# Four-stage attention kernel for 32 batches: all TensorE products as two halves of 64 partitions, in two lanes

## What is computed

```python
# stage 1: attention, 16 heads of 16, queries from the side input, keys from x and the own position
q = (side + b_self) @ Wq + bq;  k = ((x + b_prev) | (side + b_self)) @ Wk + bk;  v = (x | side) @ Wv + bv
w = softmax(cat(masked(q @ k_prev.T), sum(q * k_self)) / 4)
x = x + (w[:, :-1] @ v_prev + w[:, -1:] * v_self) @ Wo + bo
# stage 2: adapter chosen by an id, then layer norm
a = x + relu(x @ W1[id] + b1[id]) @ W2[id] + b2[id];  x = x + normed(a) * gamma[id] + beta[id]
# stage 3: a linear layer chosen by an id
x = x + x @ W[id].T + b[id]
# stage 4: pooling by scores, under one of three masks
s = tanh(x @ W1 + b1) @ v
x = x + (softmax(where(mask[id], s, NEG)) @ x) / count
```

## Time and profile before

| | |
|---|---|
| median of 3 runs | 934.45 us (933.97 to 934.48) |
| the profiled execution | 936.64 us, its span 935.0 us |
| a step of the loop | 27.44 us (489.60 to 517.04) |
| TensorE, VectorE, ScalarE, GpSimd busy | 97%, 75%, 68%, 64% of the span |
| TensorE's clock | upper level (2.4 GHz) in all 40 slices |
| DMA | 124.54 MB, mean 133 GB/s |

### The profile page before, as it was taken

One profiled execution on the slowest core, in us unless ns is written; L12 is line 12 of the kernel. 1 busy time (PEld: TensorE's weight loads), 2 busy tenths in 40 slices (PEclk: granted clock), 3 DMA queues, 4 the chain that ended last, 5 costly groups with the idle time before them and its releaser, 6 DMA issues.

```text
span 935.0 us, 27514 instructions
## 1 busy us (share of the span) xinstructions
PE 910.3 (97%) x8611; PEld 762.3 (82%) x8611; DVE 704.2 (75%) x1364; ACT 634.4 (68%) x1125; POOL 600.9 (64%) x767
## 2 busy tenths in 40 slices
PE   8999999999999999999999999999999999999887
PEld 7787788888888888888888888888888888887666
DVE  7666777787777787777788777787877777787555
ACT  3456677777667677767777776777776677776643
POOL 4354667767666676666767666677766667764562
PEclk9999999999999999999999999999999999999999
DMA  7444433445443444444344444334444433433231
GB/s 246 152 141 143 136 116 125 145 138 159 141 129 102 151 133 145 160 132 125 107 159 129 149 159 125 124 115 154 135 149 149 121 125 128 152 116 96 71 95 53
DMA packets 113208, 124.54 MB, mean 133 GB/s; under 512 B 23541, under 2 KB 95110, under 8 KB 113158
## 3 DMA queue, kind: packets, MB, share of 16 engines
q1 hardware_dynamic: 111384, 121.22, 41.3%
q10 hardware_dynamic: 1774, 2.68, 0.9%
HBM read 63.99 MB, written 8.96 MB: 78 GB/s over the span
## 4 chain that ended last, share of the span: by engine, by line
PE 89%; issue 5%; DVE 3%; ACT 2%; POOL 1%; DVEq 0%; POOLq 0%; ACTq 0%
PE M L482 28%; PE ST L585 12%; PE PV L564 11%; PE PV L482 10%; PE M L490 7%; PE SN L589 6%; PE M L804 5%; PE M L616 3%; PE M L674 3%; DVE mx L1343 2%; PE M L763 2%; PE M L753 1%; ACT x1T L1029 1%; PE M L497 1%; PE M L641 0%
## 5 line engine op out<-in xcount | busy, mean ns | idle before, releaser
L1343 DVE TENSOR_REDUCE mx<-SN 128x4 f32<-128x1024 f32 x248 | 303.6, 1224 | 102.0 <-PE SN L589 99.4
L1053 ACT ACTIVATE pt<-ST 128x1024 f32<-128x1024 f32 x256 | 262.5, 1025 | 105.0 <-PE ST L585 95.0
L585 PE MATMUL ST<-qst,kst 64*128 64x256 f32 x1024 | 187.7, 305 | 8.6 <-ACT pt L1053 3.5
L585 PEld LDWEIGHTS ST<-qst,kst 64*128 64x128 f32 x1024 | 136.1, 186 | 64.4 <-issue 26.9
L589 PE MATMUL SN<-kst,qst 63*128 63x256 f32 x1008 | 184.0, 304 | 0.7 <-issue 0.7
L589 PEld LDWEIGHTS SN<-kst,qst 63*128 63x128 f32 x1008 | 132.8, 186 | 1.3 <-issue 0.9
L564 PE MATMUL PV<-pt,vaug 128*32 128x256 f32 x2048 | 124.6, 384 | 0.1
L888 POOL TENSOR_TENSOR ss<-xsin,ss 128x512 fp32r<-128x512 f32 x32 | 41.0, 1283 | 122.2 <-ACT ss L1029 114.3
L564 PEld LDWEIGHTS PV<-pt,vaug 128*32 128x32 f32 x2048 | 60.2, 110 | 43.6 <-issue 6.3
L888 POOL TENSOR_TENSOR x2T<-x2f,x2T 128x512 fp32r<-128x512 f32 x31 | 39.9, 1288 | 47.0 <-ACT x2T L1029 47.0
L482 PE MATMUL M<-lwp,x2T 128*128 128x320 f32 x378 | 68.2, 316 | 1.0 <-issue 1.0
(11 more groups left out here) (190 smaller groups left out, 2101.4 us busy)
## 6 DMA issues: line engine op xcount, KB each, us to landing
qst<-qp SPq DMA_DIRECT2D x186, 128.0 KB
kst<-kp SPq DMA_DIRECT2D x186, 128.0 KB
xsin<-in_xsT SPq DMA_DIRECT2D x31, 512.0 KB, 3.4
adw<-in_wad SPq DMA_DIRECT2D x32, 322.5 KB, 3.8
xr<-in_x SPq DMA_DIRECT2D x32, 256.0 KB, 4.1
lwf<-in_lwT SPq DMA_DIRECT2D x32, 256.0 KB, 3.1
pm<-in_pmask SPq DMA_DIRECT2D x31, 257.0 KB, 2.7
out<-ob SPq DMA_DIRECT2D x31, 256.0 KB, 2.2
```

The costliest lines, as they stand in the source:

```text
L585: keys = nc.tensor.matmul(ST[e][:, half * S:half * S + S], kst[par][lo_:lo_ + MROW + 1, pair, half * P:half * P + P], qst[par][lo_:lo_ + M ...
L1053: nc.scalar.activation(pt[:, g, :, j:j + 2, :].rearrange("p h e q -> p e h q"), ST2[:].rearrange("p e (h q) -> p e h q", h=2), ACT.Exp, sc ...
L1343: nc.vector.tensor_reduce(out=mx[odd][:, :, col:col + PH + 1:PH].rearrange("p h e -> p e h"), in_=SN2[:].rearrange("p e (h k) -> p e h k", ...
```

## The change

From step 3 on (`LANES_FROM`) up to step 31 (`LANES_TO` = 32) all engines run a new function `lane_step` in place of `step`; the tail takes over what is left. Steps -2 to 2 are as before.

On TensorE every product and transpose other than scores and weighted sums is cut into two halves along the contraction, partitions 0 to 63 (LOW) and 64 to 127 (HIGH). Both halves add into the same bank, one first and the other later; the second waits on a semaphore (`half_low`, `half_high`) which the first half's last matmul increments. `LANES` holds for each piece its step offset, its bank and which half goes first. `side_by_side` takes two generators, a low lane and a high one, and issues from the lane that has used fewer columns so far, so that two different pieces run beside each other. A transpose's half turns 64 partitions into 64 output columns. `rest(n)` issues nothing; it only counts columns. `weighted` pv1 of batch t-1 now stands first in the step, pv0 ahead of scores 6 as before. The scores blocks are unchanged.

The other engines' queues have the same operations in a new order, and some a step later: the high part `x1Thi`, `x1Tlo` and `x1bT` of batch t-2, `x3` of t-3, `masked`, pooling and `outs` of t-4 are now done in step t. `pool` is two pieces with a bank each. VectorE now waits for both halves of `lin` before either `x3`. The tail gets `masked`, `x3`, `r3`, `outs` of one more batch on VectorE, `srep`, `lin0`, `lin1`, `pT`, `pool` on TensorE (with 8 fillers in place of 10 at one point), and the exponential and its copy on ScalarE.

```diff
+LANES = [
+    ("pv1", -1, 3, None), ("x1T", -2, 1, LOW), ("srep", -4, 2, HIGH), ("v", 1, 0, HIGH), ("ks", 1, 3, LOW),
+    ("h", -2, 2, HIGH), ("k", 2, 1, HIGH), ("num0", -1, 0, LOW), ("num1", -1, 3, LOW), ("q", 2, 2, HIGH),
+    ("ad", -2, 0, LOW), ("pT", -4, 3, LOW), ("aT", -1, 1, HIGH), ("ss", 1, 3, LOW), ("pool0", -4, 0, HIGH),
+    ("pool1", -4, 2, LOW), ("lin0", -3, 1, LOW), ("lin1", -3, 3, HIGH), ("pv0", 0, 2, None), ("x2T", -2, 3, LOW),
+    ("wo", -1, 0, HIGH), ("vs", 1, 1, LOW),
+]
...
+            def side_by_side(low, high):
+
+                halves_left, spent = [low, high], [0, 0]
+                while halves_left != [None, None]:
+                    k = HIGH if halves_left[LOW] is None else LOW
+                    if None not in halves_left:
+                        k = LOW if spent[LOW] <= spent[HIGH] else HIGH
+                    columns = next(halves_left[k], None)
+                    if columns is None:
+                        halves_left[k] = None
+                    else:
+                        spent[k] += columns
...
+                def other_half(name, b):
+
+                    while name not in issued:
+                        yield 64
+                    pe.wait_ge(sem(HALF[LANES[LANE[name]][3]]), halves(name, b))
...
+                def split_rows(name, dsts, left, right, rows):
+
+                    begins, r, last = first_half(name, rows), rows_of(rows), None
+                    for k, dst in enumerate(dsts):
+                        for c in range(NC2):
+                            for x, y in SPLIT:
+                                last = nc.tensor.matmul(dst, left(x, c, k)[r], right(y, c)[r],
+                                                        start=begins and k == c == x == y == 0,
+                                                        stop=not begins and c == 1 and x == 1, skip_group_check=True)
+                                yield dst.shape[-1]
+                    return last
+
+                def turned_rows(dst, src, cols, rows):
+
+                    r, last = rows_of(rows), None
+                    for to, at in cols:
+                        last = nc.tensor.transpose(dst[:, to + 64 * rows:to + 64 * rows + 64], src(at)[r], ident[r, r])
+                        yield 134
+                    return last
...
+                if by_lanes("pv1", t - 1):
+                    vacate("pv1", t - 1)
+                    weighted(lane_bank["pv1"], 1, t - 1, odd)
+                scores(on, t, par, 0)
+                side_by_side(itertools.chain(residual_turned(t - 2, LOW), rest(256), row_scores(t - 4, LOW),
+                                             own_keys(t + 1, odd, LOW)),
+                             itertools.chain(row_scores(t - 4, HIGH), values(t + 1, odd, HIGH),
+                                             residual_turned(t - 2, HIGH)))
+                scores(on, t, par, 1)
+                side_by_side(itertools.chain(values(t + 1, odd, LOW), rest(2000), hidden(t - 2, LOW),
+                                             queries_back(0, t - 1, LOW), queries_back(1, t - 1, LOW)),
+                             itertools.chain(own_keys(t + 1, odd, HIGH), hidden(t - 2, HIGH), keys_(t + 2, par, HIGH)))
+                scores(on, t, par, 2)
+                side_by_side(itertools.chain(keys_(t + 2, par, LOW), adapted(t - 2, LOW), pooled_turned(t - 4, LOW),
+                                             queries(t + 2, par, LOW)),
+                             itertools.chain(queries_back(0, t - 1, HIGH), queries_back(1, t - 1, HIGH),
+                                             queries(t + 2, par, HIGH), rest(1000), pooled_turned(t - 4, HIGH),
+                                             adapted(t - 2, HIGH), attention_turned(t - 1, HIGH)))
+                scores(on, t, par, 3)
+                side_by_side(itertools.chain(own_scores(t + 1, LOW), attention_turned(t - 1, LOW), pooled(1, t - 4, LOW)),
+                             itertools.chain(pooled(0, t - 4, HIGH), rest(300), own_scores(t + 1, HIGH)))
+                scores(on, t, par, 4)
+                side_by_side(itertools.chain(pooled(0, t - 4, LOW), linear(0, t - 3, LOW)),
+                             itertools.chain(pooled(1, t - 4, HIGH), linear(1, t - 3, HIGH)))
+                scores(on, t, par, 5)
+                side_by_side(linear(1, t - 3, LOW), linear(0, t - 3, HIGH))
+                vacate("pv0", t)
+                weighted(lane_bank["pv0"], 0, t, par)
+                scores(on, t, par, 6)
+                side_by_side(itertools.chain(normed_turned(t - 2, LOW), own_values(t + 1, odd, LOW)),
+                             itertools.chain(attention_out(t - 1, HIGH), normed_turned(t - 2, HIGH)))
+                scores(on, t, par, 7)
+                side_by_side(attention_out(t - 1, LOW), own_values(t + 1, odd, HIGH))
```

More of the change, by code:

```diff
@@ L72 @@
 NAMES = [n for _, n, _, _ in PIECES]
+LOW, HIGH = 0, 1
+HALF = ("half_low", "half_high")
+LANES_FROM, LANES_TO = 3, B
+LANES = [
[5 more added lines that the diff above has]
+]
+LANE = {n: k for k, (n, _, _, _) in enumerate(LANES)}
+STEP_OF = {n: o for _, n, o, _ in PIECES}
+STEP_OF.update(pool0=STEP_OF["pool"], pool1=STEP_OF["pool"])
 def done(b, per=1, nth=None):
@@ L92, in before, with by_lanes, halves @@
     return b * UNITS + unit
+def by_lanes(name, b):
+    return not isinstance(b, int) or max(0, LANES_FROM + STEP_OF[name]) <= b < B
+def halves(name, b):
+    _, off, _, first = LANES[LANE[name]]
+    u = b - off
+    own = [(o + (1 if j <= LANE[name] else 0), max(0, LANES_FROM + STEP_OF[m]))
+           for j, (m, o, _, f) in enumerate(LANES) if f == first]
+    if isinstance(u, int):
+        return sum(max(0, min(u + a, B) - start) for a, start in own)
+    return u * len(own) + sum(a - start for a, start in own)
 def block4(nc: bass.Bass, x, xsT, lens, ids, wq, wk, wv, wo, wad, lw, lwT, lb, fixed_d, early_d, kidx_d,
@@ L459, in _ @@
+            steps(sp, step, lane_step)
             step(B, 0, "lwf")
@@ L461, in _ @@
             step(B, 0, "pm")
+            step(B - 1, 1, "out")
             step(B, 0, "lbr")
@@ L524, in _, with weighted @@
                       "lin0": (("x3", 2, 1),), "lin1": (("x3", 2, 2),), "srep": (("masked", 1, 1),),
[1 row of a table removed]
[2 rows of a table added]
                       "pv1": (("pvt", 2, 2),)}
+            def weighted(dst, k, b, i):
+                pe.wait_ge(sem("exp_done"), before(b, 8 * k + 8))
+                pe.wait_ge(sem("v"), done(b))
+                for g in (2 * k, 2 * k + 1):
+                    for kb in range(2):
+                        for j in range(4):
+                            last = nc.tensor.matmul(dst[32 * j:32 * j + 32, (g % 2) * S:(g % 2) * S + S],
+                                                    vaug[i][:, kb, 4 * g + j, :], pt[:, g, kb, j, :],
+                                                    start=kb == 0, stop=kb == 1)
+                last.then_inc(sem("pv_done"), 1)
@@ L554, in free @@
                             return
-                def weighted(k, b, i):
-                    pe.wait_ge(sem("exp_done"), before(b, 8 * k + 8))
-                    pe.wait_ge(sem("v"), done(b))
-                    free(f"pv{k}")
-                    for g in (2 * k, 2 * k + 1):
-                        for kb in range(2):
-                            for j in range(4):
-                                last = nc.tensor.matmul(PV[32 * j:32 * j + 32, (g % 2) * S:(g % 2) * S + S],
-                                                        vaug[i][:, kb, 4 * g + j, :], pt[:, g, kb, j, :],
-                                                        start=kb == 0, stop=kb == 1)
-                    last.then_inc(sem("pv_done"), 1)
@@ L718, in step @@
                     pe.wait_ge(sem("ones1"), 32)
-                scores(0)
+                scores(on, t, par, 0)
                 if go("E", "pv1"):
-                    weighted(1, t - 1, odd)
+                    free("pv1")
+                    weighted(place("pv1", t), 1, t - 1, odd)
                 first = isinstance(t, int) and t == 0
@@ L769, in step @@
                     keys_()
-                scores(4)
+                scores(on, t, par, 4)
                 if on["B"]:
@@ L786, in step @@
                 if on["C"]:
-                    weighted(0, t, par)
-                scores(6)
+                    free("pv0")
+                    weighted(bank["pv0"], 0, t, par)
+                scores(on, t, par, 6)
                 if go("F", "x2T"):
@@ L831, in keep_busy @@
+            steps(pe, step, lane_step)
             def keep_busy(n):
@@ L1009, in _ @@
+            steps(pool, step, lane_step)
             step(B, 0, "eyed")
@@ L1563, in _ @@
+            steps(dve, step, lane_step)
+            step(B - 1, 1, "masked")
+            step(B - 1, 1, "x3a")
             step(B, 0, "x3b")
@@ L1571, in _ @@
             step(B - 1, 1, "x1Tlo")
+            step(B - 1, 1, "r3")
             step(B, 0, "sc")
```

(1 more changed line is left out.)

848 lines of the change are left out of this document (774 added, 74 removed), and 3 rows, old and new, of the table READER.

## The result

The changed kernel takes **955.61 us** (median; 952.26 to 958.21) against 934.47 (933.97 to 936.46) of the kernel before on the same chip: ratio **1.022**, 95% interval 1.0178 to 1.0263. I had forecast 890 with a range up to 926. It is slower where I said faster, and the profiled execution (953.38, span 951.6) shows why in four lines of its page.

A forecast was written before the change was run, and what follows sets the result against it. TensorE was taken as the bound, busy 27.42 of a 27.44 us step. Its 24.6 us plus 1.2 of stalls make 25.8; 936.64 - 47.6 + 3.0 = 892.0, less 2.2 for the median, about 890 us, range 862 to 926.

The forecast's parts named there:

- 29 x 1.64: Steps 3 to 31 each get 1.64 us shorter, 47.6 us in all.
- Halves' own cost: Second halves' semaphore waits and the extra increment for each group of transposes, costed at nothing.
- Borders: Around scores blocks, switching between full and half rows costs 0.37 us a block; eight blocks save 3.0 us a step.
- Products and transposes: In TensorE's lanes, half products cost 0.119 us, pairs' sum unchanged; half transposes cost 0.056, saving 1.4 us a step.
- D: Rival: mixed lanes wait for each other in TensorE's queue; at 30 ns a pair, step 29.2, time 990 us; chance 0.07.
- C: Rival: half transposes cost 0.109 us, so lanes gain nothing there; step 26.8 us, near 919; chance 0.19 together with B.
- E: Rival: halves' weight loads are not hidden, so the 15.6 us of products and transposes nearly double; chance 0.02.
- B: Rival: VectorE's queue order binds, four fullest periods lose 0.25 us more each; step 26.8, 919 us; chance 0.19 with C.
- F: Rival: a bank's reader is late in every section, TensorE waits instead of switching, time stays near 934; chance 0.05.
- A: Rival: nearly no stalls, step 24.6 to 25.1 us, time 862 us; chance 0.14.
- The step of 25.8: Main-loop step: TensorE alone 24.6 us plus 1.2 of stalls, the largest 0.74 ahead of scores 3; 1.64 less than before.
- Ends: First steps stay; the tail takes on a pooling and a linear layer, costing 3 us, bounds 0 and 4.

The follow-up runs named there:

- written out: The changed kernel with TensorE's program alone written out for all steps instead of looping, other engines keeping their loops; 899.95 us, ratio to before 0.9612.
- written out, end filled: The changed kernel with TensorE's program written out, plus useless half products where steps 30 and 31 have nothing to compute; 893.11 us, ratio 0.9552.
- the run with 1.6 us less work on TensorE: The changed kernel, loop kept, with half products vs, wo and v issuing only the first of their three part products; 898.5 us.

## Why the prediction was wrong

Spans in us, by the first scores start of steps 3 and 31; the forecast's are worked out from before (104.2, 768.4, 62.5) with its own terms:

| | up to step 3 | steps 3 to 30 | step 31 and tail | span |
|---|---|---|---|---|
| before | 104.2 | 768.4 | 62.5 | 935.0 |
| forecast | 104.2 | 768.4 - 28 x 1.64 = 722.5 | 62.5 - 1.6 + 3 = 63.9 | 890.6 |
| changed kernel | 105.4 | 779.0 | 67.1 | 951.6 |
| written out | 105.6 | 725.7 | 67.1 | 898.4 |
| written out, end filled | 105.4 | 720.9 | 64.7 | 891.0 |

**The step that failed** is the sum's "29 x 1.64". It takes the steps of the loop to be like those outside, and rests on "Halves' own cost", which I put at nothing and where I asked only what a half waits for; the loop's 22 steps took 625.5 us where the sum has 567.5. That 26 transposes become 52, and each of the full products two, means 605 more instructions in the body of a hardware loop; I counted matmuls by their start distances and never as instructions that must be there. The page of before had the queue (27 blocks) and I did not ask why it was so little for 33 steps. None of the rivals had this mechanism, and the chance of 0.11 for slower stood on others.

*Borders:* right in kind; a block's 0.37 was not measured by itself, the full-row matmul put ahead of it costs 0.31. *Products and transposes:* right, 0.12 and 0.06 us. *Weighted:* a little high: a block takes 1.86 us to the next start, as before, and enters 0.21 to 0.26 behind the last start, so some 1.97 and not 2.08. **D**, the slower side, got the sign and nothing else: mixed pairs keep 0.12 us. **C** and **E** fall with the same rows. **B** and **F** fall with the steps outside the loop, **A** too: even the run with 1.6 us less work on TensorE keeps steps of 25.5.

*The step of 25.8:* measured 25.65 (25.88 every second time while the other engines loop), but by two errors that cancel, and so by luck. Walked from scores 0, the written-out kernel's step at 543.4 has its scores at 2.63, 6.61, 10.96, 13.70, 16.20, 19.63, 21.94 and 25.85 us, against my 2.24, 6.39 and 11.17 for the first three and 25.8 for the end. Yet TensorE is busy for 25.68 of 25.80, and the 0.74 us wait ahead of scores 3 isn't there. VectorE's timeline in that step:

```profile
551.08 0.18 DVE L2330 TENSOR_TENSOR tot<-M,eself 128x16 f32<-128x16 f32 x1 [1.66 <-PE M L1027]
...
552.17 0.10 DVE L2391 TENSOR_TENSOR sc<-sum,pm 128x2 f32<-128x2 f32 x1
552.32 0.17 DVE L2393 RECIPROCAL r<-sc 128x2 f32<-128x2 f32 x1
552.48 1.23 DVE L2298 TENSOR_REDUCE mx<-SN 128x4 f32<-128x1024 f32 x1
```

The numerators start at 7.70 (I had 7.67), but `sc3` takes 0.10 us and not the 0.98 of the earlier trace rows, so the reduction starts at 9.10 and not at 9.87. The lanes in turn are fuller than my 24.6 by some 0.7 us: the longer lane of a section isn't all of it, since both lanes are issued in one order and a lane waits inside a section too, as here within section 3, where 0.44 us lie between two starts of TensorE:

```profile
555.72 0.22 PE L1027 MATMUL M<-fixed,nv 64*128 64x64 f32 x1
556.16 0.28 PE L1125 MATMUL PV<-fixed,pr 64*128 64x16 f32 x1
```

A sum can be right with its terms wrong; the walk shows it, the total doesn't.

*Ends:* with the clock up, the tail plus step 31 is 64.7, 0.8 above the forecast's 63.9, so the +3 was a fair size; with the clock down it is 67.1. That the clock falls when steps 30 and 31 run thin was not priced, as the last line of the forecast admits, nor were the 1.2 us at the change from old to new steps. The first is worth the 6.8 us that filling took off the written-out kernel. In the changed kernel itself step 30 keeps the upper level (25.30 us from 859.10 to 884.40), and only the tail has 10.2 us at the lower.

So of the 61.0 us between the forecast's span and the changed kernel's, 58.0 are in the 22 steps of the loop (625.5 where the forecast's terms give 603.6 - 22 x 1.64 = 567.5), 3.2 in step 31 and the tail, 1.2 ahead of step 3, less 1.4 in the six new steps outside the loop. Without the loop the same steps take 567.8 us, so the loop's part is the jumps. The rest of the 65.6 between 890 and 955.6 is what medians differ from profiled executions, 2.2 us on either side, and rounding.

## What to carry to other kernels

Before a change multiplies instructions inside a hardware loop, count one body of each engine in instructions (matmuls, loads, waits and register work) and look at the instruction queue of the page: silent during the loop means held, blocks in every pass mean that each jump back will wait. If the new body might be too large, write that engine's program out, since straight code was fetched without delay here, or shorten the body before anything else is tuned. And walk a step by its intermediate times: an end that fits proves neither the floor nor the waits.

## What the runs showed of the hardware

**A loop's body.** 1144, 1444, 1557 and 1685 instructions were kept by TensorE, 1749, 2274 and 3481 were not. A jump that isn't held costs 5.6 to 7.3 us. Most of it is idle time (3.2 and 0.9 in the timeline above), the rest longer matmuls, in part at the lower clock: in the changed kernel a pass takes 51.5 us written out, 56.6 and 57.1 with a jump and the clock up, 58.1 and 58.2 in the three with 6.8 us at the lower level. The Trainium skill, Runtime: NRT & Kernel Launch, section Instruction fetch mechanics, says that instructions are refilled in 16 KiB blocks of 256, and that a taken branch whose target lies outside a window of two such blocks stalls for a fetch. The 16 KB packets and the idle time agree; a window of two blocks doesn't, since bodies of up to 1685 instructions, 6.6 blocks, jumped back without a packet. It also gives TensorE room for 2048 instructions; a body of 1749 should then be held, and it was not.

**Small operations of VectorE beside GpSimd.** `sc3` has two columns; it took a mean of 1003 ns before and 97 ns in the written-out lanes, and the maxima's `mneg` 471 and 215:

```profile
L1506 DVE TENSOR_TENSOR sc<-sum,pm 128x2 f32<-128x2 f32 x18 | 18.1, 1003 | 0.0
L1319 DVE SCALAR_TENSOR_TENSOR mneg<-mx,nself 128x16 fp32r<-128x16 f32 x36 | 17.0, 471 | 2.0
```

```profile
L2309 DVE SCALAR_TENSOR_TENSOR mneg<-mx,nself 128x16 fp32r<-128x16 f32 x38 | 8.2, 215 | 2.1
L2391 DVE TENSOR_TENSOR sc<-sum,pm 128x2 f32<-128x2 f32 x19 | 1.8, 97 | 0.0
```

(The first two are of before, the others of the written-out kernel, 300 to 790 us: count, busy us, mean ns, idle.) In the kernel before, GpSimd runs this beside the `sc3` of the earlier trace rows, which starts at 505.21 and takes 0.98 us:

```profile
505.12 1.06 POOL L969 TENSOR_TENSOR tv<-vself,eself 128x512 f32<-128x512 f32 x1
```

Both end at 506.18 or 506.19. Of the 32 `sc3`, 27 are long (0.98 us and more) and 26 of these end 15 to 18 ns behind an operation of GpSimd; the other five take 0.16 us at most. The new order has them apart. `sc3` and `mneg` together are 40 us shorter over the run (58.5 and 18.2), about all that VectorE's busy time fell (704.2 to 665.4 and 664.4), so that its 21.6 us a step, which the prediction kept, became 20.2. Both inputs of `sc3` lie in SBUF; the Trainium skill, SBUF — State Buffer, section Who interferes with whom, says that such an operation of VectorE contends with a GpSimd operation that reads SBUF, and that the port pair they share is an exclusive lock. The trace agrees. No run here was made for it alone, so it is argued from coincidence of ends. A duration read from one row can hold a neighbour's.

**Increments.** 150 dense increments a step on TensorE's queue lengthened it from 27.4 to 36.0 us, 57 ns each on average: none at the start of a group of products, 0.09 us each where products with two between them start 0.30 apart instead of 0.12. 14 scattered ones cost (891.6 - 889.3) / 29 = 0.08 us a step. That work queued ahead hides the first ones fits both, and is not shown by itself.
